# Two graph layers on one core: the attention context of the step before is issued directly behind the turns

## The reference, cut to what matters

```python
h = jnp.maximum(_layernorm(x, axis=-1), 0.0)
...
q = _heads(seq_inputs @ Wq + bq)
k = _heads(seq_inputs @ Wk + bk)
v = _heads(seq_inputs @ Wv + bv)
scores = jnp.einsum('bhqd,bhkd->bhqk', q, k) / np.sqrt(HEAD_SIZE)
bias = jnp.where(graph_mask, 0.0, NEG)[:, None]
probs = jax.nn.softmax(scores + bias, axis=-1)
ctx = jnp.einsum('bhqk,bhkd->bhqd', probs, v)
```

## Time and profile before

| what | value |
|---|---|
| median of 3 runs | 1903.73 us (1902.87 to 1903.93) |
| profiled execution, own time | 1904.39 us |
| profiled execution, span from the first to the last instruction | 1902.6 us |
| mean granted TensorE clock | 0.992 of 2.4 GHz |
| PE busy | 1778.2 us, 93% |
| DVE, ACT, POOL busy | 71%, 58%, 54% |
| HBM traffic | 24 GB/s |

### The profile page before, as it was taken

The page is one execution under the profiler, slowest core; times in us unless marked ns, Lnnn a source line. Parts: engine busy times, 40 slices in busy tenths (PEclk is TensorE's granted clock), DMA queues, the critical chain, the costliest instruction groups (busy, mean ns, idle before and its releaser), DMA issues.

```text
span 1902.6 us, 36049 instructions
## 1 busy us (share of the span) xinstructions
PE 1778.2 (93%) x10992; PEld 1073.8 (56%) x10992; DVE 1347.1 (71%) x3114; ACT 1101.0 (58%) x2215; POOL 1034.6 (54%) x1287
## 2 busy tenths in 40 slices
PE   6899999999999999999999999999999999999985
PEld 4565646557464564646657465574646646465561
DVE  4678577776767767677775777767677676776846
ACT  3566555665555656556665556655556565566643
POOL 4256464564556546465564645645565564654635
PEclk9899999999999999999999999999999999999998
DMA  4000100001010010100001010010100101000000
GB/s 147 18 17 11 46 6 33 22 8 41 6 50 6 12 37 6 50 6 29 21 13 42 6 33 22 12 38 6 50 6 12 37 6 50 6 17 18 9 9 17
DMA packets 38112, 46.43 MB, mean 24 GB/s; under 512 B 2624, under 2 KB 38080, under 8 KB 38080
## 3 DMA queue, kind: packets, MB, share of 16 engines
q1 hardware_dynamic: 38080, 46.03, 7.6%
HBM read 33.44 MB, written 12.58 MB: 24 GB/s over the span
## 4 chain that ended last, share of the span: by engine, by line
PE 65%; DVE 14%; issue 8%; ACT 6%; POOL 5%; DVEq 1%; DMA 0%; ACTq 0%; POOLq 0%
PE score L1073 13%; PE work L1073 13%; PE acc L1211 7%; PE acc L1156 7%; PE score L1130 7%; PE work L1141 6%; PE acc L1215 6%; DVE arena L848 4%; ACT arena L563 3%; PE acc L1175 2%; POOL arena L432 2%; POOL arena L439 2%; PE score L1196 2%; DVE stats L759 2%; DVE xres L829 2%
## 5 line engine op out<-in xcount | busy, mean ns | idle before, releaser
L848 DVE SCALAR_TENSOR_TENSOR arena<-score,uqT,adjT 128x512 f32<-128x512 f32 x576 | 392.4, 743 | 80.8 <-PE acc L1215 41.0
L405 POOL TENSOR_SCALAR arena<-arena,rinv 128x512 f32<-128x512 f32 x384 | 281.6, 751 | 209.4 <-DVE rinv L810 209.4
L563 ACT ACTIVATE arena<-sm,nmax 128x512 f32<-128x512 f32 x384 | 273.3, 713 | 148.4 <-DVE nmax L804 147.3
L439 POOL TENSOR_TENSOR arena<-arena,adjT 128x512 f32<-128x512 f32 x192 | 224.1, 1167 | 157.6 <-ACT arena L603 153.2
L804 DVE CUSTOM_DVE_ANT_0 sm<-score,mask 128x512 f32<-128x512 f32 x384 | 247.9, 686 | 76.5 <-PE score L1130 75.2
L1141 PEld LDWEIGHTS work<-ident_f,arena 128*128 128x128 f32 x1536 | 168.7, 141 | 146.5 <-DVE arena L814 77.6
L1141 PE MATMUL work<-ident_f,arena 128*128 128x128 f32 x1536 | 219.9, 281 | 25.1 <-DVE arena L859 18.5
L1211 PE MATMUL acc<-arena 128*32 128x512 f32 x1536 | 203.8, 602 | 39.6 <-DVE arena L848 21.6
L1156 PE MATMUL acc<-arena,v_tok 128*64 128x512 f32 x768 | 199.8, 613 | 6.2 <-DVE arena L814 6.2
L600 ACT ACTIVATE arena<-score,nqT 128x512 f32<-128x512 f32 x192 | 130.1, 678 | 122.8 <-PE score L1196 92.6
L1215 PE MATMUL acc<-arena,u_den 128*3 128x512 f32 x1536 | 200.9, 592 | 0.0
(11 more groups left out here) (163 smaller groups left out, 3915.3 us busy)
## 6 DMA issues: line engine op xcount, KB each, us to landing
x_in<-in_x SPq DMA_DIRECT2D x16, 768.0 KB, 4.7
xb<-in_x SPq DMA_DIRECT2D x16, 768.0 KB, 4.5
out_x<-xres SPq DMA_DIRECT2D x64, 192.0 KB, 1.9
adj_u<-in_adj SPq DMA_DIRECT2D x16, 256.0 KB, 2.8
arena<-in_wk SPq DMA_DIRECT2D x1, 576.0 KB, 5.9
arena<-in_wq SPq DMA_DIRECT2D x1, 576.0 KB, 6.9
arena<-in_wv SPq DMA_DIRECT2D x1, 576.0 KB, 8.0
arena<-in_wf SPq DMA_DIRECT2D x1, 576.0 KB, 8.8
```

Source lines behind the costliest of these rows:

```text
L405: nc.gpsimd.tensor_scalar(pr, pr, rinv[:, p, t, i:i + 1], 1.0, ALU.mult, ALU.mult).then_inc(probs_ready, 1)
L439: nc.gpsimd.tensor_tensor(edge[:, (n * HG + HG - 1) % 8], t_ring[:, n % 2], adjT[:, n % TT], ALU.mult).then_inc(last_edge_ready, 1)
L563: nc.scalar.activation(probs[p % 2 * 2 + i][:, t], sm[:, n % NSM], ACT.Exp, scale=-1.0, bias=nmax[:, p, t, i:i + 1], accum_out=rsum[:, p, ...
L848: nc.vector.scalar_tensor_tensor(out=edge[:, (n * HG + j) % 8], in0=score[j][:], scalar=uqT[:, c, q:q + 1], in1=adjT[:, c], op0=ALU.max, o ...
```

## The change

Within a step, the context of the step before is issued directly behind the turns. What stood between the two (score tiles, normed turns, a key product) now stands behind the context. The context of c = 3, the key products behind a pair, the tables `S_AFTER`, `NORM_AFTER` and `KEY_AFTER`, and the order on the other engines stay as they are.

```diff
                 for p in range(NPAIR):
                     for c in range(TT):
                         turn_probs(g, p, c)
+                        if c > 0:
+                            context(g, p, c - 1)
                         for tile in S_AFTER.get((p, c), ()):
                             scores(g, *tile)
                         if more:
...
                                 turn_norm(g + 1, 0, t)
                             if (p, c) in KEY_AFTER:
                                 query_key(g + 1, KEY_AFTER[p, c], "k")
-                        if c > 0:
-                            context(g, p, c - 1)
                     context(g, p, TT - 1)
                     if more and p in KEY_BEHIND:
                         if p == 1:
```

## The result

The changed kernel takes 1933.63 us (median of 4 runs, 1931.72 to 1934.06) against 1903.30 of the kernel before: a ratio of 1.0158, 95% interval 1.014 to 1.0175. It is 30 us slower. The forecast was 1926.4 with a range of 1917 to 1936; the rival in which DVE and POOL collide gave 1934.1.

The account below looks back on a forecast made before the run. The prediction took TensorE (PE), busy 93% of the span, as the bound. It added 16 graphs x 1.42 = 22.7 us to the profiled 1904.39, giving 1927.1, less 0.66 to the median: 1926.4 us, range 1917 to 1936.

Parts of the forecast that it names:

- DVE and POOL collide: Rival: line 867's second call meets POOL's line 449; 0.5 us more, 1.9 a graph, 1934.1 us; chance 0.19.
- second chain: From late scores(2,3) through DVE and ACT to DVE's copy of turns(1,3) and context(1,3): 1.42 us late, including the earlier 1.0.
- 16 graphs x 1.42 = 22.7: Forecast's whole loss in us: context(1,3) 1.42 us late in each of 16 graphs.
- I cost both at nothing: Steps (0,1) and (0,2): scores(1,3) 1.01 us late, but its maxima had about 0.6 in hand; no loss.
- up to 0.4 us more a graph: Extra loss allowed for steps (0,1) and (0,2) if the cover is gone.
- the upper rival: The rival DVE and POOL collide, 1934.1 us, chance 0.19; extra loss at (0,1) and (0,2) was said to lie within it.
- line 867 at its second place takes over 1 us: Sign that the forecast is wrong: DVE's line 867, between maxima of (2,0) and (2,1), takes over 1 us.
- the plain shift: Main forecast: late score tiles delay DVE, ACT and PE by 1.42 us a graph, 1926.4 us; chance 0.58.
- may itself start 0.4 later: In DVE and POOL collide: POOL's addition of line 449 may start 0.4 us later, then ending at 646.4.
- "less" and "more": Graph 0 probably loses less and graph 15 more than the others; both were left at 1.42 us.
- swallowed the second chain: Rival: DVE reaches scores(2,3) earlier or norm copies gain; 1.0 us a graph remains, 1919.7 us; chance 0.15.
- cost no clock: Rival denied here: each new PE gap brings 3 us at half clock, about 1.5 more a graph, 1950.4 us; chance 0.02.

Follow-up runs that it names:

- e1: Kernel before with the context moved in front only in step (0,3): 1912.97 us, ratio 1.0050.
- e2: Kernel before with the context moved in front only in step (1,1): 1908.58 us, ratio 1.0031.
- e3: The change in all its steps but (0,1), whose score tile stays in front of the context: 1926.52 us, ratio 1.0119.
- e9: Kernel before with the context moved in front only in steps (0,2) and (1,2): 1904.04 us, ratio 1.0003.
- e11: Changed kernel with line 867's first call before maxima(1,3), scores(2,3) before turns(1,1), DVE's copy of turns(1,3) before the norm's low parts: 1904.79 us.
- e4: Kernel before with the context moved in front only in step (0,1): 1911.84 us, ratio 1.0046.
- e8: Kernel before with DVE's copy of turns(1,3) before the norm's low parts and ACT's copy of turns(0,1) before the exponentials of (1,2): 1894.66 us.
- e5: Changed kernel with line 867's first call on DVE in front of maxima(1,3): 1927.45 us, ratio 1.0126.

## Why the prediction was right and where it fell short

**Right: the direction, its cause and the place.** The score tiles are late by one context (1.01 us, as taken), this passes through DVE's maxima and ACT's unbroken row of work to turns(1,1), and a second time through scores(2,3). Only the end of this second chain was one place off: PE meets it at turns(1,3), over ACT's copy of turns(1,2), and context(1,3) keeps the wait of 0.44 that it had. In the changed kernel the second half of turns(1,1) is 1.43 us late against turns(0,0), that of turns(1,3) 1.76, context(1,3) 1.80. e1 and e2 show the two chains singly and e3 both together, with 9.96, 5.6 and 23.5 us; "16 graphs x 1.42 = 22.7" is the cost of the steps (0,2), (0,3), (1,1) and (1,2), and e3 is just these, with 1.33 a graph.

**Right: what costs nothing.** No new wait stands at a moved context, the normed turns are free (e9), pair 2 and layer 2 are as before (but for the clock in the last graph, last section), and PE's own additional 0.15 us in step (0,3) is covered by the wait at turns(1,1). Without that wait (e11) it may not be.

**Wrong: "I cost both at nothing" for steps (0,1) and (0,2).** The cover for scores(1,3) was there for PE, but not for DVE: line 867 behind these maxima is issued 0.45 us later. That was enough to lose its place to a POOL operation, at 0.66 us for its end. The prediction named the possibility, with "up to 0.4 us more a graph", and gave it to the upper rival; measured, the step (0,1) costs 0.47. The late tile should have been followed to the next operation of DVE that can be held up by POOL.

**The rival that came.** "DVE and POOL collide" had 0.19 and gave 1934.1; measured 1933.63. Its price was meant as 0.5 us for line 867 at its second place; the trace shows 1.01 us against 0.57, its end 1.58 later (14.39 to 15.97 after turns(0,0)), against the rival's 1.5. By this the prediction's own sign of being wrong, "line 867 at its second place takes over 1 us", came true: the plain shift is not the whole mechanism, and 1926.4 is 7.2 us low. That 1933.63 lies in the range is owed to the rival, which the range was drawn to take in. The rival assumed that line 449 "may itself start 0.4 later" without saying why; it is 0.49 later, because of the collision at the first place, which the prediction didn't foresee; so the rival's closeness to the measured time is partly luck. Without that (e3) line 449 starts at 14.05, as before, the second call takes 0.65 and the rival doesn't come. The rule of the Trainium skill (SBUF — State Buffer, "SBUF: two separate sides"), an exclusive lock under which the later one stands still until the other is over, gave this outcome, and the trace agrees: the calls above that started within a POOL operation end 0.41 to 0.43 us after it, however long they waited.

**The sum, graph by graph.** From one turns(0,0) to the next it is 117.24 us against 115.43 between graphs 1 and 14, 1.81 a graph and not 1.42. Graph 0 lost 0.88 (it has no line 867), and the attention of graph 15 lost 2.24; "less" and "more" were right, though graph 0 varies by more than this between executions (its distance is 31.83 before and 31.25 in e4). The distance from turns(0,3) to context(1,3) was foreseen as 16.1 and is 16.36; ACT's wait before the exponential of (2,0) as 2.2 and is 2.29. The wait at turns(1,1) was foreseen as one for ACT's copies, near 0.9; it is 0.77 for DVE's and 0.17 for ACT's, as the delay reaches this place over DVE's own order of work too (maxima, line 867, maxima, copy), and not over ACT alone. The sum, 0.94, is as foreseen.

**The other rivals.** Nothing swallowed the second chain; PE's gaps of up to 0.8 us cost no clock in the attention (granted 1.00 over its 40 us). No part of the change gained time.

## What to carry to other kernels

When work on the bounding engine is reordered, what counts is not whether the moved instructions must wait but who waits for what now comes later: follow the delayed results through the other engines to the next place at which the bounding engine needs them back, and compare with the slack there (here 0.08 us). A growing delay may be met at another place than the wait that is already in the list. A context was pulled forward that nobody was waiting for, in front of score tiles that head a chain of four engines. Slack covers only once: two delays that are each partly covered alone (0.60 and 0.33 us) cost 1.33 together. And where a DVE operation has to wait for POOL's, as line 867 here, a delay of a few tenths is not passed on as it is: the operation has to be set against POOL's timetable, since it ends either as planned or 0.4 us after POOL's operation. A delay of 0.45 us became 0.66 there, and a gain of 0.33 became 0.01. Last, an edit that wins the time back is to be tried on the kernel before as well, or it proves less than it seems.

## What was not expected of the hardware

The last graph's layer 2 lost another 1.5 us. Of this 0.9 lie behind a place where PE waits three times for the norm, in both kernels alike, and then the granted clock is half. Windows of the kernel before, then of the changed one (columns as in rows 3):

```profile
1829.00:1833.00 4.00, 0.59 (x5) 0.39 (x4) 2.11 (x5) 2.56 (x6) 2.30 (x3) 0.96 0.00 0
1833.00:1836.50 3.50, 3.50 (x9) 2.77 (x10) 0.00 (x0) 0.00 (x0) 3.31 (x6) 0.56 0.02 5
```
```profile
1858.00:1862.00 4.00, 1.42 (x5) 1.14 (x6) 1.52 (x4) 1.95 (x4) 3.15 (x4) 0.68 0.01 4
1862.00:1866.00 4.00, 4.00 (x11) 3.04 (x10) 0.00 (x0) 0.68 (x2) 2.66 (x5) 0.50 0.00 0
```

The products behind the waits follow one another in 0.43 us at half clock (1.2 GHz) and 0.23 at full (2.4). Before, this lasts from 1832.95 to about 1836; after, from 1861.10 to about 1866, although the waits ahead are the same. The other 0.6 us lie in the last 62 us, where PE's last products ran at a granted clock of 0.84 before (1884.6 to 1888.6) and of 0.50 in the changed kernel (1914.3 to 1918.3).

The length of the first of these stretches doesn't follow the change: it is about 3 us in e9 and over 5 in e8, with a wait of 1.51 us ahead in both. From this wait to the L1175 products it is 21.10 us in e9 and 22.30 in e11, the least and the most of the thirteen profiles. So about a microsecond between two runs can come from it. More comes from the start of the program: the second graph's attention begins between 167.25 us (e4) and 170.04 us (e5), and not in the order of the medians. Differences of one or two microseconds between two profiled runs are therefore not to be explained by the edit; the distances within one graph, which I used above, don't contain them. What decides the length of a stretch at half clock wasn't tried.
